# One gated feed-forward kernel replaced by another: transposes by DMA, whole-tile PSUM reads, x prepared in units of up to four tiles

## The reference

```python
si = einsum('bnd,d->bn', ctx, W[0, :128]); sj = einsum('bnd,d->bn', ctx, W[0, 128:])
xatt = 0.6 * sigmoid(si[:, :, None] + sj[:, None, :] + b) + 0.4 * layernorm(x)
x = x + tanh(g_xattn) * xatt
def bitlinear(x, w):                      # rms norm, 8-bit rows, ternary weights
    xn = x * rsqrt(mean(x * x) + 1e-6)
    s = 127 / clip(max(abs(xn)), 1e-5);   xq = clip(round(xn * s), -128, 127) / s
    t = 1 / clip(mean(abs(w)), 1e-5);     wq = clip(round(w * t), -1, 1) / t
    return xq @ wq.T
n = layernorm(x)
x = x + tanh(g_ffn) * bitlinear(silu(bitlinear(n, w1)) * bitlinear(n, w2), w3)
```

## Time and profile before

| | |
|---|---|
| median of 3 runs | 197.76 us (197.4 to 199.41) |
| the profiled execution | 198.57 us, of which the span is 196.8 us |
| mean granted clock of PE | 0.991 of 2.4 GHz |
| instructions | 3146 |
| HBM read, written | 13.90 MB, 4.19 MB |
| w1's scale complete | 22.2 us |
| first `hidden` (L738) | 55.7 us |
| last operation of DVE ends | 194.29 us |

### The profile page before, as it was taken

One profiled execution on the slowest core, in us unless ns is written; L12 is line 12 of the kernel. 1 busy time (PEld: TensorE's weight loads), 2 busy tenths in 40 slices (PEclk: granted clock), 3 DMA queues, 4 the chain that ended last, 5 costly groups with the idle time before them and its releaser, 6 DMA issues.

```text
span 196.8 us, 3146 instructions
## 1 busy us (share of the span) xinstructions
PE 159.7 (81%) x994; PEld 88.3 (45%) x994; DVE 141.1 (72%) x276; ACT 139.6 (71%) x224; POOL 135.0 (69%) x248
## 2 busy tenths in 40 slices
PE   0170597975999589898998989898999999989773
PEld 0140474743555245454454544444355455444440
DVE  0079565676883946679798998989895665689761
ACT  3019678999799758997897979779785674646620
POOL 2043999999989988879788887879766235246520
PEclk9999999999999969999999999999999999999999
DMA  2499999730000100031403030110101011010121
GB/s 65 149 400 368 387 360 410 261 100 13 0 3 0 53 0 3 0 107 57 145 15 107 2 107 5 53 53 0 57 0 53 11 47 53 0 53 2 67 96 53
DMA packets 10976, 18.29 MB, mean 93 GB/s; under 512 B 1488, under 2 KB 3536, under 8 KB 10960
## 3 DMA queue, kind: packets, MB, share of 16 engines
q1 hardware_dynamic: 10960, 18.09, 26.2%
HBM read 13.90 MB, written 4.19 MB: 92 GB/s over the span
## 4 chain that ended last, share of the span: by engine, by line
POOL 51%; PE 25%; issue 7%; ACT 5%; DVE 5%; DMA 3%; SPq 2%; DVEq 0%; POOLq 0%; ACTq 0%
PE ps L1002 12%; PE ps L1042 9%; POOL raw L360 8%; POOL raw_room L377 7%; POOL xn_ring L345 5%; POOL raw_room L360 4%; POOL xn_ring L351 4%; POOL ln_r L316 4%; POOL rnorm L341 3%; DMA b_col<-in_L_xattn_b_dram 3%; PE ps L1029 2%; POOL h_r L368 2%; POOL ln_nu L319 2%; POOL x_ring L332 2%; POOL ln_ve L315 2%
## 5 line engine op out<-in xcount | busy, mean ns | idle before, releaser
L1002 PE MATMUL ps<-w1T,xqT 128*128 128x512 f16 (+1 forms) x192 | 46.1, 367 | 1.7 <-ACT g_ring L501 0.8
L1002 PE MATMUL ps<-w2T,xqT 128*128 128x512 f16 (+1 forms) x192 | 46.2, 371 | 0.5 <-DVE raw_room L738 0.5
L738 DVE SCALAR_TENSOR_TENSOR raw_room<-ps,deq,g_ring 128x512 f32<-128x512 f32 (+1 forms) x48 | 32.9, 700 | 15.4 <-PE ps L1002 12.2
L1042 PE MATMUL ps<-w3T,raw_room 128*128 128x512 f16 x176 | 40.6, 379 | 2.5 <-ACT raw_room L520 2.3
L501 ACT ACTIVATE g_ring<-ps,deq 128x512 f32<-128x512 f32 (+1 forms) x48 | 31.1, 655 | 10.6 <-PE ps L1002 6.8
L377 POOL TENSOR_SCALAR raw_room<-raw_room,h_scale 128x1408 f32<-128x1408 f32 x15 | 24.7, 1644 | 8.9 <-DVE h_scale L753 8.9
L1002 PEld LDWEIGHTS ps<-w1T,xqT 128*128 128x128 f16 x192 | 18.2, 99 | 19.9 <-ACT g_ring L501 1.6
L510 ACT ACTIVATE junk<-raw_room 128x1408 f16<-128x1408 f32 x16 | 22.0, 1374 | 7.1 <-DVE raw_room L738 7.1
L1002 PEld LDWEIGHTS ps<-w2T,xqT 128*128 128x128 f16 x192 | 18.0, 100 | 19.1 <-DVE raw_room L738 1.8
L520 ACT ACTIVATE raw_room<-ps 128x1024 f16<-128x1024 f16 (+1 forms) x31 | 22.2, 769 | 5.7 <-PE ps L1029 4.8
L745 DVE TENSOR_REDUCE h_max<-raw_room 128x1 f32<-128x1408 f32 x16 | 25.8, 1615 | 0.3
(11 more groups left out here) (80 smaller groups left out, 253.5 us busy)
## 6 DMA issues: line engine op xcount, KB each, us to landing
x_ring<-in_x_dram SPq DMA_DIRECT2D x16, 256.0 KB, 3.1
out_dram<-out_ring SPq DMA_DIRECT2D x16, 256.0 KB, 2.0
raw<-in_L_ffn_w_dram SPq DMA_DIRECT2D x4, 704.0 KB, 10.4
raw_room<-in_L_ffn_w_dram SPq DMA_DIRECT2D x3, 768.0 KB, 9.3
raw<-in_L_ffn_w_dram SPq DMA_DIRECT2D x3, 768.0 KB, 11.8
x_all<-in_ctx_dram SPq DMA_DIRECT2D x4, 256.0 KB, 9.6
raw_room<-in_L_ffn_w_dram SPq DMA_DIRECT2D x1, 512.0 KB, 11.4
raw<-in_L_ffn_w_dram SPq DMA_DIRECT2D x1, 512.0 KB, 11.4
```

The costliest lines, as they stand in the source:

```text
L738: v.scalar_tensor_tensor(out=h_ring[:, t % 3, lo:hi], in0=ps_up[n % 2][:, 0:hi - lo], scalar=deq[:, t, 1:2], in1=gate[:, t % 4, lo:hi], op ...
L1002: last = m.matmul(bank[n % 2][:, 0:hi - lo], xqT[:, i % XQ, k, :], wT[w][:, k, lo:hi], start=(k == 0), stop=(k == KD - 1))
L1042: last = m.matmul(ps_y[:, :], hqT[:, t % 2, k, :], wT[2][:, k, :], start=(k == 0), stop=(k == KH - 1))
```

## The change

The file is replaced by another of the same structure and names. What it does differently:

- The last product's operand and x from tile 4 on are transposed by DMA: SP issues `dma_start_transpose` for w3's four row blocks (`turn_w3`), for 15 tiles of h (`turn_h`, 128x1408 f16) and for 12 of x (`turn_x`). PE transposes only w1, w2, the first four tiles of x and the last tile of h.
- The raw weights are no longer rounded by an added constant: conversion scales them down to where f16 rounds them (`conv_w`, with TINY = 2^-24), on DVE for nine groups of w1 and w2 and on POOL for three and for w3; four of the PSUM groups are evacuated by DVE.
- Gate and up have three PSUM banks each, not two of one. `silu` and `hidden` read all 1408 columns at once. Gate of the next tile waits for the silu of this one, up for the hidden of this one. The rings: 4 tiles of gate, 4 of h, 3 of quantised h, 4 of its transposed form, 8 of transposed x, 3 outputs.
- x is kept whole in `c_all` and prepared in `UNITS` of 1, 1, 2, 2, 2, 4 and 4 tiles: factors (`scale_x`, `dequant_gate`, `dequant_up`), x1 (`make_x`) and its maximum (`max_x`) are one operation for a unit. The mean is taken off x1 before it is kept, and comes back as the bias of ACT's `finish`; DVE adds x1 in `add_x`, except for the last two tiles.
- Scores: products of the context with W on POOL (`products`) and row sums on DVE in place of the transposes and matmuls on PE; four small inputs are loaded to one partition by ACT's DMA queue and spread by one matmul.
- Loads: w1's third piece is the first, all of w1 ahead of w2, and one tile of x with it.

The core of the diff:

```diff
-PRE = 3
-XQ = 6
-AHEAD = 3
+    UNITS = [(0, 1), (1, 2), (2, 4), (4, 6), (6, 8), (8, 12), (12, 16)]
+    BY_PE = 4
+    CONV_DVE = [[0, 1, 2, 3, 4, 5], [0, 2, 4], []]
+    CONV_POOL = [[], [1, 3, 5], [0, 1, 2, 3]]
+    OUT_DVE = [[2, 4], [2, 4]]
+    OUT_ACT = [[0, 1, 3, 5], [0, 1, 3, 5]]
...
+            def turn_x(i):
+                sp.wait_ge(xq_done, i + 1)
+                if i >= XT:
+                    sp.wait_ge(up_ps, i - XT + 1)
+                sp.dma_start_transpose(xqT[:, i % XT, :, :], xq[:, i % XQ, :]).then_inc(xT_in[i % XQ], 16)
+
+            def turn_h(t):
+                sp.wait_ge(hq_done, t + 1)
...
+                sp.dma_start_transpose(hqT[:, t % HT, :, :], hq[:, t % HQ, :]).then_inc(hT_in[t % HQ], 16)
...
+            def quant_h(t):
+                pool.wait_ge(h_scaled, t + 1)
+                if t >= HQ:
+                    pool.wait_ge(hT_in[t % HQ], 16 * (t // HQ))
+                g.tensor_scalar(hq[:, t % HQ, :], hid[:, t % HS, :], h_scale[:, t:t + 1], TINY, ALU.mult,
+                                ALU.mult).then_inc(hq_done, 1)
...
-            def make_x1(i):
-                v.scalar_tensor_tensor(out=x1_all[:, i, :], in0=th_ring[:, i % 2, :], scalar=t03[:, 0:1],
-                                       in1=x_ring[:, i % 4, :], op0=ALU.mult, op1=ALU.add,
-                                       accum_out=x1_sum[:, i:i + 1]).then_inc(x1_done, 1)
+            def make_x(u):
+                lo, hi = UNITS[u]
+                dve.wait_ge(affine_done, hi)
+                v.scalar_tensor_tensor(out=c_all[:, lo:hi, :], in0=th_ring[:, lo % 4:lo % 4 + hi - lo, :],
+                                       scalar=t03[:, 0:1], in1=c_all[:, lo:hi, :], op0=ALU.mult,
+                                       op1=ALU.add).then_inc(made, 1)
...
+            def hidden(t):
+                dve.wait_ge(deq_up, UNIT[t] + 1)
+                if t >= HS:
+                    dve.wait_ge(hq_done, t - HS + 1)
+                dve.wait_ge(silu_done, t + 1)
+                dve.wait_ge(up_ps, t + 1)
+                v.scalar_tensor_tensor(out=hid[:, t % HS, :], in0=ps_up[:, 0:H], scalar=deq[:, 1, t:t + 1],
+                                       in1=gate[:, t % GATES, :], op0=ALU.mult, op1=ALU.mult).then_inc(h_done, 1)
...
+            def add_x(t):
+                dve.wait_ge(y_out, t + 1)
+                o = out_ring[:, t % OUTS, :]
+                v.tensor_tensor(o, o, c_all[:, t, :], ALU.add).then_inc(out_done, 1)
...
+            def gate_product(t):
+                if t >= 1:
+                    pe.wait_ge(silu_done, t)
+                product(t, 0, ps_gate, gate_ps)
...
+            def up_product(t):
...
+                    pe.wait_ge(h_done, t)
+                product(t, 1, ps_up, up_ps)
```

More of the change, by code:

```diff
@@ L941, in sum_w, with spread_row @@
[L941 to L948 removed]
+            def spread_row():
+                pe.wait_ge(row_in, 64)
+                m.matmul(ps_y[0][:, 0:2 * DC + 3], ones[0:1, :], row[0:1, :], start=True, stop=True).then_inc(spread_ps, 1)
```

1603 lines of the change are left out of this document (868 added, 735 removed).

## The result

On one chip and in the same rounds, the changed kernel takes 179.25 us (median of 4 runs, 178.51 to 180.76) and the kernel before 198.41 (4 runs, 197.4 to 199.41). The ratio is 0.904, with a 95% interval of 0.896 to 0.913: it is faster by 9.6%, 19.2 us.

What follows compares the result with a forecast made beforehand. POOL and DVE together were taken to bound the kernel from about 80 to 141 us, then PE. Three stages, 49.5 + 91.5 + 46, gave a span of 187.0 us, thus a median of 188.0, range 176 to 204.

Steps and rivals of the forecast that it cites:

- stage 2: From the first hidden product to the factors of tiles 12 to 15: 91.5 us, reckoned as DVE's work plus waits.
- Stage 1: From the span's start to the first hidden product: loads, weight scales and DVE's work, ending at 49.5 us.
- All at 0.41 make 23 us: DVE's waits for POOL in stage 2: 55 candidate operations, 9 to 23 us, taken as 16.
- the order doesn't fit: Rival: waits in the program-order queues leave 10% of stage 2 idle, 9 us more, 197, no change; chance 0.12.
- PE in stage 2: PE has 29 blocks of 2.37 us in stage 2, 69 of 91 us, so it pauses more.
- Without the waits for POOL the span would be 167: Whole span without DVE's waits for POOL, 16 and 4.2 us less than forecast.
- The unit of four: Four-tile x1 (2.3 us), maximum (2.3) and scales delay hidden products 10 and 11; costs in stage 2, not stage 3.
- Stage 3: From the factors of tiles 12 to 15 to the end: PE's remaining product blocks, last addition and store, 46 us.
- The DMA transposes: Transposes issued on SP's queue, without a row in the profile: 3.5 us taken for each.
- the slow rival: DMA transposes queue up on SP; slower than before from 6.8 us a tile of h; chance 0.12.
- The count of places: DMA transposes stand on the path at three places only, w3's, x4's and x12's; each us more costs three.
- What would show it: Signs: chain mostly DVE from 30 to 140 us, DVE busy some 150, ACT and POOL under 125, transposes 3 to 4.

## Why the prediction was right, and where it was off

**The bound before** (POOL and DVE up to 141 us, then PE) and **the forecast's sign** hold, though the chain before, from 80 to 141 us, has 47.5 us of POOL and 2.4 of DVE, so POOL's part was the larger. That the number came out inside the range is partly the range's width, 28 us: the span was 10.3 us less than the sum, 8.5 of it in stage 2. The largest share of the gain is in stage 2, the first stage gave nearly as much, PE's end little.

**Stage 1, 49.5 against 47.4.** The loads are as reckoned: w1's scale 15.2 against 15.9, w2's 31 against 30.65. The 18.4 us from w2's scale to the first hidden product (14.2 of work, 4.2 of waits) took 16.8. The waits' mechanism is there (a `th_neg` of 1.40 us, an x1 block of 2.28 against 1.28, both at 30 to 40 us), with 2.0 us of DVE standing for POOL beside it.

**Stage 2, 91.5 against 83.0.** Here is the mis-sized term. The step said "All at 0.41 make 23 us; if those standing right behind each other share one wait, there are 21 groups and 9 us. I take 16, the middle." The timeline of stage 2 has 14 operations longer than the same ones alone, 8.4 us in all, where 16 were put down. That is just under the low bound of 9, but by another count: 14 of 55 candidates and 0.60 us each, not 21 groups of 0.41. Two pairs show the mechanism, a clip beside POOL's conversion of w3 and a scale step beside POOL's rounding of h. The scale step ends when POOL's operation ends, the clip 0.4 us behind:

```profile
56.07 1.44 POOL L448 TENSOR_SCALAR hqT<-raw,w_scale 128x1408 f16<-128x1408 f32 x1
...
56.18 1.72 DVE L906 TENSOR_SCALAR hqT<-hqT 128x1408 f16<-128x1408 f16 x1
...
60.18 0.52 DVE L906 TENSOR_SCALAR hqT<-hqT 128x1408 f16<-128x1408 f16 x1
...
127.66 1.62 POOL L463 TENSOR_SCALAR hq<-raw,h_scale 128x1408 f16<-128x1408 f32 x1
...
128.07 1.23 DVE L858 TENSOR_SCALAR x_step<-xn_step 128x4 f32<-128x4 f32 x1
```

The rest of the error is in DVE's own work: 83.0 less 8.4 and less 3.1 of standing is 71.5, against 75.5 put down; so 7.6 us less of waits and 4.0 less of work, and 3.1 of standing that the sum had at nothing, make the 8.5. The clip took 0.52 (0.6 taken). Copies out of PSUM, in stage 1, took 0.67 where 1.2 was taken. Standing was 3.1 us in 83: the rival "the order doesn't fit", with 10% idle, is refuted for this order (3.1 us is 4%).

**PE in stage 2.** The step "In stage 2 of the new one PE has 29 blocks of 2.37, 69 of 91 us, so it pauses more" has the blocks right (29), and in the mean PE does pause more (busy 74.5 of 83.0 us, against 8.32 of 8.77 before). What it concealed is where: seven blocks stand before 75.5 us and 22 behind, where PE is full. The mean of a stage said slack; the windows say a second bound. The sentence "Without the waits for POOL the span would be 167" is not borne out by it: from the last product of tile 1 to the end are 101.2 us, of which PE stands for 1.64 and loses 2.3 to the slower clock, so 167 needs that product some 6 to 8 us earlier as well, and the additions taken off DVE gave 1.7 at most.

**The unit of four.** "The unit of four costs here and not in stage 3" counts its delay of hidden 10 rightly (the pause of 1.64 us at 132), but said nothing of what it saves. Against units of two it saves 8 us, of which 2.7 went with POOL's powers and some 2.3 with the one held rounding.

**Stage 3, 46 against 46.3.** Block by block as reckoned: eleven blocks from 132.18 to 158.33, 2.38 us each, against 2.37.

**The DMA transposes**, 3.5 taken:

```profile
hqT<-hq SPq DMA_TRANSPOSE x15, 3.5
xqT<-xq SPq DMA_TRANSPOSE x12, 2.4
w3T<-hqT SPq DMA_TRANSPOSE x4, 3.8
```

The price was right and the slow rival (from 6.8 us a tile of h) is out. The count of places was short: h's transpose also lands last at tile 1, where PE stands 4.53 us for it and the clock falls. By the estimate from "VectorE: DVE Perf Modes" in the Trainium skill (The three transpose paths), 14.4 us for a tile of h, the trace does not agree; its "Advanced Engine Details and Errata", X-Bar Transpose, is nearer: 256 KB of output landed in 2.2 us, the transposed 352 KB of h in 3.5 and 128 KB of x in 2.4.

**What would show it.** Right: POOL and ACT under 125 us (120.2, 105.5), transposes in 3 to 4 us, short operations of 0.2 alone and over 1.2 beside POOL. Wrong: the chain is not mostly DVE from 30 to 140 us, it has 45.9 us of DVE, 37.1 of POOL and 10.4 of PE (the rest is time between instructions), and DVE's busy time is 139.9, not 150.

## What to carry to other kernels

Reckon every engine's work in each stretch between two milestones, not over a stage: an engine with slack in the mean can be the bound in its second half, and then relief of the first one gives little. In a schedule written out by hand, count the short instructions on the fullest engine and join them over tiles: 20 more of 0.2 us cost 3.7 us of their own here, and 2 more by a collision with GpSimd that they shifted into place; 4 more long ones cost nothing. When an operation is moved earlier, read what stands between it and the next one that matters, on every queue it is moved past; the first milestone may come 3.6 us sooner and the second 1.4 later.
